# Mamba-plus-MoE layer: the state loop's exponential and pad copy are issued one step ahead

## The chip, the cores and the metric

The kernel runs as one program on all 8 cores of a Trainium2 chip. The cores exchange nothing; each works on half of one sequence. The metric is the time of the slowest core, in microseconds (us) on the device.

Names of the engines in the rows: PE is TensorE (PEld its weight loads), DVE is VectorE, ACT is ScalarE, POOL is GpSimd, SP is SyncE. Here SP only issues DMAs, and POOL only issues DMAs.

## The reference

```python
# per sequence, d_inner = 2048, 16 states, 4096 positions
xi, res = split(x @ W_in)
xi = silu(causal_conv4(xi) + conv_b)
Bm, Cm = split(xi @ W_xproj)
delta = softplus(xi @ W_dt + b_dt)
A = -exp(A_log)                                  # 16 values
def step(h, inp):
    dA = exp(d_i[:, None, :] * A[None, :, None])
    h = h * dA + d_i * B_i * u_i                 # for each of 16 states
    y_i = sum(h * C_i, axis=states)
y = (ys + xi * D_param) * silu(res)
x = layernorm(x + y @ W_out)
# then softmax router (top 2 of 16 experts of 1024x1024) + 2 shared experts
x = layernorm(x + x + routed + shared)
```

## The kernel before

**Stages.** Each core computes 4096 positions of one sequence, of which it outputs 2048. The first 2048 only bring the recurrent state to the right value (or are zeros, for the first half of a sequence). Time is cut in 16 chunks of 256 positions (TA). A position's 2048 channels lie as 16 tiles (CT) of 128 partitions, so a chunk of one quantity is a 128x4096 f32 tile. The stages are: projection and convolution (to about 790 us); the state stage, lines 496 to 742, of which this document speaks; the output projection, layernorm and router; and the mixture of experts. Barriers stand between them.

**The state stage.** Its loop is `for ch in range(NCH)` (line 620, chunks 0 to 15) around `for n in range(NST)` (line 644, steps 0 to 15, one for each state). Chunks 8 to 15 are "real" (line 622): they also produce output. A step n does this:

- ACT: `dA[n%2] = exp(A[n] * d)` (line 653), 128x4096 into one of two buffers `dA_b`. It waits until the scan that last read the buffer is done (`dA_used`, line 652).
- ACT: the pad copy (line 658). It puts the 16 state values that the chunk before left for state n (`carry`) into column 0 of every channel tile of `dBu_b`. It waits for the scan before (`prev_scan`), which read the same tile.
- DVE: `dBu = du * B[n]` (line 665), 128x4096, the rest of that tile.
- DVE: the scan (line 679) `h = dA*h + dBu` over 128x4112; it waits for the pad copy (`actn`, line 678), which is later in ACT's program than the exponential.
- ACT: the carry copy (line 685), last column of `h` into `carry`; it waits for this step's scan.
- In real chunks only, DVE: `y_acc = h * C[n]` (line 696), and PE adds it up over the states in PSUM with 8 identity matmuls (line 701).

Every engine executes its own program in order, and the helper class `Chain` (line 110) makes each DVE and ACT operation wait for its predecessor; all of their rows therefore carry line 121, and one tells them apart by tiles.

**The side work in chunks 0 to 6.** While chunk ch runs its 16 steps, PE computes `delta` of the chunks 2ch+2 and 2ch+3, in 16 groups, one issued at each step (`a2_group`, line 541): a slab of `W_dt` (1 MB in SBUF, two slab buffers) comes in by a DMA from POOL, 34 matmuls use it, and ACT evacuates the two PSUM banks (`a2_evac`, line 575) with an Exp into `g_b` and a Ln into `sres_b`. The evacuations are put into ACT's program at the head of a step, by the list `a2_target` (line 627): none at steps 0 to 3, one at each of steps 4 to 11, two at each of steps 12, 13 and 14, one at step 15, and the last one behind step 15 (line 707). The group issued at step n takes the pair of banks that evacuation n-4 frees. Evacuation 7 (at step 11) and the last one are followed by the store `d_sp<-sres_b` from POOL, ahead of the next slab loads in POOL's program. Chunk 7 has steps without side work.

**Between chunks.** SP's program has, at step 1 of a chunk that isn't real, the load of the next `u_b`, and at step 15 (lines 672 to 677): wait for the last exponential (`dfree_A`, it read `d_b`), load the next `d_b` (2 MB); wait for the last `dBu` product (`dufree_V`), load the next `Bb_b` (2 MB, 16 rows broadcast to all partitions). A next real chunk also loads `Cb_b` behind the last product (lines 713 to 717), and, after the product with `sres_b` (line 731), `u_b` and `sres_b`. The next chunk begins with `du = d * u` on DVE (line 637), which waits for all of these loads at once (`ev_cur`).

Of the kernel before, what the change touches and what calls it, by code (L numbers as in the profile page):

```python
# [12 lines left out]
AF = mybir.ActivationFunctionType  # L13
# [4 lines left out]
NST = 16  # L18
# [7 lines left out]
CT = C2 // 128  # L26
# [102 lines left out]
def build_nc(debug=False, phases=5):  # L129
# [39 lines left out]
    A_bc = sb("A_bc", [128, NST], F32)  # L169
# [14 lines left out]
    carry = sb("carry", [128, NST * CT], F32)  # L184
# [12 lines left out]
    cA = Ctr(es, nc, "cA")  # L197
    cV = Ctr(es, nc, "cV")
# [8 lines left out]
    def emit(_):  # L207
        te = nc.tensor
        ve = Chain(nc.vector, cV)
        se = Chain(nc.scalar, cA)  # L210
# [57 lines left out]
        def emit_ln(in_b, out_b, W, sq_b, stat, mu_bc, rs_bc):  # L268
# [14 lines left out]
            for dt_i in range(DT):  # L283
# [47 lines left out]
                            in_=W_in.rearrange("(k p) c -> p k c", p=128)[:, :, 0:C2]), 16)  # L331
        cL.inc(ge.dma_start(out=wres[:].rearrange("p (k c) -> p k c", c=C2),
                            in_=W_in.rearrange("(k p) c -> p k c", p=128)[:, :, C2:2 * C2]), 16)
        cL.inc(ge.dma_start(out=cvd[:].rearrange("p (i n) -> p i n", n=128),
                            in_=convd.rearrange("i p n -> p i n")), 16)
        cL.inc(ge.dma_start(out=wxp[:].rearrange("p (k c) -> p k c", c=32),
                            in_=W_xproj.rearrange("(k p) c -> p k c", p=128)), 16)
# [4 lines left out]
                            in_=b_dt.rearrange("(c p) -> p c", p=128),  # L342
                            allow_slow_non_contiguous=True), 16)
        cS.inc(sy.dma_start(out=cvb_c[:],
                            in_=conv_b.rearrange("(c p) -> p c", p=128),
                            allow_slow_non_contiguous=True), 16)
        cS.inc(sy.dma_start(out=Dp_c[:],
                            in_=D_param.rearrange("(c p) -> p c", p=128),
                            allow_slow_non_contiguous=True), 16)
        cS.inc(sy.dma_start(out=bsum_c[:],  # L350
                            in_=bs[0].rearrange("(c p) -> p c", p=128),
                            allow_slow_non_contiguous=True), 16)
        cS.inc(sy.dma_start(out=bs_t[:],
                            in_=bs[1].rearrange("(c p) -> p c", p=128),
# [5 lines left out]
                            in_=centT.rearrange("(k p) c -> p k c", p=128)), 16)  # L360
# [33 lines left out]
        for ch in range(NCH):  # L394
            bi = ch % 2
            if xcons[bi]:
                ge.wait_ge(cT.sem, xcons[bi])
            cL.inc(ge.dma_start(
                out=xcb[bi][:].rearrange("p (k t) -> p k t", t=TA),
                in_=xT.rearrange("(k p) t -> p k t", p=128)[:, :, ch * TA:(ch + 1) * TA]), 16)  # L400
# [21 lines left out]
            for cp in range(CT // 2):  # L422
                b = acquire2()
                for ct in (2 * cp, 2 * cp + 1):
# [13 lines left out]
                    in_=pairview(b, TA), func=AF.Silu))  # L438
# [59 lines left out]
        TAp = TA + 1  # L498
# [121 lines left out]
        for ch in range(NCH):  # L620
            a2_done = 0
            real = ch >= NRE
            ev_cur = ev_next
            if ch <= NRE - 2:
                a2_sched = [(2 * ch + 2, mp) for mp in range(CT // 2)] + \
                           [(2 * ch + 3, mp) for mp in range(CT // 2)]
                a2_target = [0, 0, 0, 0, 1, 2, 3, 4, 5, 6, 7, 8, 10, 12, 14, 15]
            else:
                a2_sched = None
            if ch == NRE:  # L630
                zmm_T = a2st['mmend']
                ve.wait_ge(cS.sem, consts_S)
                ve.wait_ge(cA.sem, cA.n)
                cV.inc(ve.tensor_scalar_mul(carry[:], carry[:], flag_col[:]))
                prev_scan = cV.n
            ve.wait_ge(*ev_cur)
            cV.inc(ve.tensor_mul(du_b[:], d_b[:], u_b[:]))
            dumult_V = cV.n
            se.wait_ge(*ev_cur)
            se.wait_ge(cV.sem, pad_V)  # L640
            if ch + 1 < NCH:
                rB.begin()
            dA_used = [0, 0]
            for n in range(NST):
                if a2_sched is not None:
                    while a2_done < a2_target[n]:
                        a2_evac(*a2evacs.pop(0))
                        a2_done += 1
                    a2_group(*a2_sched[n])
                pi = n % 2  # L650
                if dA_used[pi]:
                    se.wait_ge(cV.sem, dA_used[pi])
                cA.inc(se.activation(out=dA3[pi][:, :, 1:TAp], in_=d3,
                                     func=AF.Exp, scale=A_bc[:, n:n + 1]))
                if n == NST - 1:
                    dfree_A = cA.n
                se.wait_ge(cV.sem, prev_scan)
                cA.inc(se.activation(
                    out=dBu3[:, :, 0:1],
                    in_=carry[:, n * CT:(n + 1) * CT].rearrange("p (c o) -> p c o", o=1),  # L660
                    func=AF.Copy))
                actn = cA.n
                bview = Bbc[:, n * TA:(n + 1) * TA].rearrange(
                    "p (o t) -> p o t", o=1).broadcast_to([128, CT, TA])
                cV.inc(ve.tensor_tensor(dBu3[:, :, 1:TAp], du3, bview, ALU.mult))
                if n == 1 and ch + 1 < NCH and not real:
                    syE.wait_ge(cV.sem, dumult_V)
                    rB.dma(syE, out=u_b[:], in_=u_sp[ch + 1])
                if n == NST - 1:
                    dufree_V = cV.n  # L670
                    if ch + 1 < NCH:
                        syE.wait_ge(cL.sem, a2_spill[ch + 1])
                        syE.wait_ge(cA.sem, dfree_A)
                        syE.wait_ge(cV.sem, dumult_V)
                        rB.dma(syE, out=d_b[:], in_=d_sp[ch + 1])
                        syE.wait_ge(cV.sem, dufree_V)
                        bchain(syE, Bb_b, 0, ch + 1)
                ve.wait_ge(cA.sem, actn)
                cV.inc(ve.tensor_tensor_scan(out=h_b[:], data0=dA_b[pi][:],
                                             data1=dBu_b[:], initial=0.0,  # L680
                                             op0=ALU.mult, op1=ALU.add))
                scan_V = cV.n
                prev_scan = scan_V
                se.wait_ge(cV.sem, scan_V)
                cA.inc(se.activation(
                    out=carry[:, n * CT:(n + 1) * CT].rearrange("p (c o) -> p c o", o=1),
                    in_=h3[:, :, TA:TAp], func=AF.Copy))
                dA_used[pi] = cV.n
                if real:
                    cview = Cbc[:, n * TA:(n + 1) * TA].rearrange(  # L690
                        "p (o t) -> p o t", o=1).broadcast_to([128, CT, TA])
                    if zmm_T:
                        ve.wait_ge(cT.sem, zmm_T)
                    if n == 0:
                        ve.wait_ge(*ev_cur)
                    cV.inc(ve.tensor_tensor(y3, h3[:, :, 1:TAp], cview, ALU.mult))
                    if ch == NRE and n == 0:
                        te.wait_ge(cA.sem, a2st['lastA'])
                    te.wait_ge(cV.sem, cV.n)
                    for zb in range(8):  # L700
                        cT.inc(te.matmul(  # L701
                            PP[:, zb * 512:(zb + 1) * 512],
                            sid128[:], y_acc[:, zb * 512:(zb + 1) * 512],
                            start=(n == 0), stop=(n == NST - 1)),
                               1 if zb == 7 else 0)
                    zmm_T = cT.n
            while a2evacs:
                a2_evac(*a2evacs.pop(0))
            if ch + 1 < NCH:
                if ch + 1 == NRE:  # L710
                    syE.wait_ge(cL.sem, a2st['spill'])
                    rB.dma(syE, out=sres_b[:], in_=sres_sp[NRE])
                if ch + 1 >= NRE:
                    if ch + 1 == NRE:
                        syE.wait_ge(cT.sem, a2st['mmend'])
                    syE.wait_ge(cV.sem, cV.n if real else dufree_V)
                    bchain(syE, Cb_b, NST, ch + 1)
            if real:
                ve.wait_ge(cT.sem, zmm_T)
                ve.wait_ge(*ev_cur)  # L720
                for ct in range(CT):
                    cV.inc(ve.scalar_tensor_tensor(
                        out=y_acc[:, ct * TA:(ct + 1) * TA],
                        in0=u_b[:, ct * TA:(ct + 1) * TA],
                        scalar=Dp_c[:, ct:ct + 1],
                        in1=PP[:, ct * TA:(ct + 1) * TA],
                        op0=ALU.mult, op1=ALU.add))
                if ch == NRE:
                    ve.wait_ge(cA.sem, a2st['lastA'])
                ve.wait_ge(cL.sem, gspill_L)  # L730
                cV.inc(ve.tensor_mul(g_b[:], y_acc[:], sres_b[:]))
                ge.wait_ge(cV.sem, cV.n)
                cL.inc(ge.dma_start(out=g_sp[ch], in_=g_b[:]), 16)
                gspill_L = cL.n
                if ch + 1 < NCH:
                    syE.wait_ge(cV.sem, cV.n)
                    rB.dma(syE, out=u_b[:], in_=u_sp[ch + 1])
                    rB.dma(syE, out=sres_b[:], in_=sres_sp[ch + 1])
            if ch + 1 < NCH:
                ev_next = rB.tok()  # L740
# [336 lines left out]
```

## Time and profile before

| | us |
|---|---|
| time, median of 2 runs | 8084.86 (8078.89 to 8090.82) |
| the profiled execution, slowest core | 8089.99 |
| its span in the trace (core 6) | 8088.4 |
| spans of the 8 cores | 8016.9 to 8088.4 |
| busy: DVE / PE / ACT / POOL | 4786.4 / 3794.7 / 1400.7 / 247.2 |

The profile is one execution, seen on the slowest core. "Busy" counts the time in which an engine executes; a row's "idle before" is the time in which the engine stood still ahead of the instruction, with the instruction or transfer that ended the wait behind the arrow. A DMA's time "to landing" runs from its issue to its last byte. The span holds all but 1.6 us of the profiled execution's time.

### The profile page before, as it was taken

To read this page: it belongs to the slowest core of one execution; us is meant where nothing else is said; L and a number is where in the kernel's file an instruction comes from. 1 tells how busy PE (TensorE), PEld (TensorE's weight loads), DVE (VectorE), ACT (ScalarE), POOL (GpSimd) and SP (SyncE) were. 2 spreads that over 40 slices of the span, in tenths; PEclk is the share of its full clock that TensorE was granted. 3 is DMA by queue.
4 is the path that set the end of the run, shared out by engine and by line. 5 is a ranking of instruction groups with operands and counts; after the bars stand their busy time and mean duration, and the time that the engine had idled before them with its cause. 6 is when DMAs were issued, how large, how long until landed. Compare 5 with 4: busy or idle time off the path is not lost.

```text
span 8088.4 us, 43746 instructions; the slowest of 8 cores (8016.9 to 8088.4 us)
## 1 busy us (share of the span) xinstructions
PE 3794.7 (47%) x16512; PEld 2020.6 (25%) x16512; DVE 4786.4 (59%) x1408; ACT 1400.7 (17%) x1270; POOL 247.2 (3%) x252
## 2 busy tenths in 40 slices
PE   3887332232232230344353433535345567676767
PEld 2776221122222220111121211212111123232332
DVE  0211086686687679779797987979773322322222
ACT  0111032232232232112121121212110000000000
POOL 0000000000000000000000000000000000000000
PEclk9998676666666665667676766767667779888888
DMA  6433877576656760130202112020212067676665
GB/s 100 110 115 124 117 119 103 89 107 101 116 82 109 114 99 10 42 57 0 57 0 57 21 36 57 0 57 12 45 48 67 36 122 129 113 127 123 117 128 101
DMA packets 468236, 640.80 MB, mean 79 GB/s; under 512 B 33886, under 2 KB 361950, under 8 KB 448046
## 3 DMA queue, kind: packets, MB, share of 16 engines
q0 software_dynamic: 380816, 352.01, 28.6%
q1 hardware_dynamic: 87214, 285.99, 14.7%
q8 instruction: 135, 2.21, 0.1%
q14 instruction: 71, 0.58, 0.0%
HBM read 796.49 MB, written 134.87 MB: 115 GB/s over the span
## 4 chain that ended last, share of the span: by engine, by line
DVE 50%; DMA 20%; PE 15%; ACT 7%; another core or an unknown queue 5%; issue 3%; SPq 1%; DVEq 0%; ACTq 0%; POOLq 0%; POOL 0%
DVE h_b L121 27%; DVE dBu L121 9%; DMA wr<-WrT 9%; DVE y_acc L121 8%; ACT dAb L121 4%; PE PP L981 3%; DMA sres_b<-sres_sp 2%; PE PP L412 2%; DMA wr<-WsT 1%; PE PP L467 1%; PE PP L802 1%; PE PP L427 1%; DMA Cb_b<-W_dt 1%; DMA gbc_b<-gbc_b 1%
## 5 line engine op out<-in xcount | busy, mean ns | idle before, releaser
L121 DVE TENSOR_TENSOR_SCAN h_b<-dAb,dBu 128x4112 f32<-128x4112 f32 x256 | 2233.6, 8725 | 246.1 <-ACT dBu L121 226.1
L701 PE MATMUL PP<-y_acc,sid 128*128 128x512 f32 x2048 | 1192.5, 748 | 1831.9 <-DVE y_acc L121 1831.9
L563 PE MATMUL PP<-y_acc,Cb_b 128*128 128x256 bf16 x4096 | 681.4, 339 | 1512.6 <-DMA Cb_b<-W_dt 862.6
L121 DVE TENSOR_TENSOR dBu<-du_b,Bb_b 128x4096 f32<-128x4096 f32 x256 | 1132.8, 4425 | 26.7
L701 PEld LDWEIGHTS PP<-y_acc,sid 128*128 128x128 f32 x2048 | 488.4, 246 | 2535.5 <-issue 2535.5
L121 ACT ACTIVATE dAb<-d_b,A_bc 128x4096 f32<-128x4096 f32 x256 | 950.5, 3713 | 792.9 <-DMA sres_b<-sres_sp 414.4
L981 PE MATMUL PP<-ue,wr 128*128 128x512 bf16 x4096 | 923.4, 388 | 211.5 <-DVE ue L121 112.5
L563 PEld LDWEIGHTS PP<-y_acc,Cb_b 128*128 128x128 bf16 x4096 | 486.3, 121 | 1683.9 <-issue 1541.1
L981 PEld LDWEIGHTS PP<-ue,wr 128*128 128x128 bf16 x4096 | 404.4, 100 | 732.1 <-issue 279.3
L121 DVE TENSOR_TENSOR y_acc<-h_b,Cb_b 128x4096 f32<-128x4096 f32 x128 | 566.5, 4426 | 13.7 <-DVE h_b L121 0.5
L121 ACT ACTIVATE carry<-h_b 128x16 f32<-128x16 f32 x256 | 58.7, 229 | 2927.7 <-DVE h_b L121 2927.7
L121 DVE TENSOR_TENSOR du_b<-d_b,u_b 128x4096 f32<-128x4096 f32 x16 | 70.8, 4425 | 754.2 <-DMA Bb_b<-bc_hbm 489.9
L121 DVE SCALAR_TENSOR_TENSOR ue<-u_b,ones,gbc_b 128x4096 bf16<-128x4096 f32 x32 | 143.5, 4484 | 380.8 <-PE PP L981 260.2
L121 DVE SCALAR_TENSOR_TENSOR ue<-u_b,ones,u2b_b 128x4096 bf16<-128x4096 f32 x32 | 143.5, 4484 | 369.1 <-PE PP L981 355.5
L412 PE MATMUL PP<-xcb,wi 128*128 128x256 bf16 x2048 | 249.6, 288 | 150.5 <-DMA xcb<-xT 116.3
L121 DVE CAST xiraw<-PP 128x512 bf16<-128x512 f32 x128 | 88.5, 692 | 371.8 <-DMA sres_sp<-sres_b 189.1
L121 ACT ACTIVATE sres_b<-u_b 128x4096 f32<-128x4096 f32 x4 | 14.5, 3616 | 1463.2 <-DMA ffnin_sp<-u_b 1463.2
L412 PEld LDWEIGHTS PP<-xcb,wi 128*128 128x128 bf16 x2048 | 209.9, 103 | 189.4 <-issue 155.9
L97 POOL DMA_DIRECT2D Cb_b<-W_dt x128 | 146.4, 1145 | 1501.0 <-PE PP L567 1500.1
L121 DVE SCALAR_TENSOR_TENSOR u_b<-PP,bsum_c,u_b 128x512 f32<-128x512 f32 x32 | 24.0, 750 | 236.6 <-PE PP L981 233.3
L427 PE MATMUL PP<-xiraw,cvd 128*128 128x256 bf16 x1024 | 141.0, 272 | 20.0 <-DVE xiraw L121 20.0
L121 ACT ACTIVATE u_b<-PP 128x512 f32<-128x512 f32 x128 | 76.4, 597 | 337.5 <-PE PP L431 337.2
(104 smaller groups left out, 1963.9 us busy)
## 6 DMA issues: line engine op xcount, KB each, us to landing
Cb_b<-W_dt POOLq DMA_DIRECT2D x128, 1024.0 KB, 12.1
wr<-WrT POOLq DMA_DIRECT2D x64, 2048.0 KB, 14.8
u_sp<-u_b SPq DMA_DIRECT2D x20, 2048.0 KB, 7.4
u_b<-u_sp SPq DMA_DIRECT2D x20, 2048.0 KB, 18.5
d_sp<-sres_b POOLq DMA_DIRECT2D x16, 2048.0 KB, 11.9
d_b<-d_sp SPq DMA_DIRECT2D x16, 2048.0 KB, 9.5
Bb_b<-bc_hbm SPq DMA_DIRECT2D x16, 2048.0 KB, 41.6
xib_sp<-xib_b SPq DMA_DIRECT2D x16, 1024.0 KB, 8.7
```

Of the source, the lines that this page charges most:

```text
L97: eng.dma_start(**k).then_inc(self.sems[self.i], 16)
L121: inst = fn(*a, **k)
L412: cT.inc(te.matmul(pb[bb][:, 0:TA], wi[:, kt * C2 + mt * 128: kt * C2 + (mt + 1) * 128], xcb[bi][:, kt * TA:(kt + 1) * TA], start=(kt == 0 ...
L427: cT.inc(te.matmul(pb[bb][:, 0:TA], cvd[:, (tap * 16 + ct) * 128:(tap * 16 + ct + 1) * 128], xr3[:, ct, tap:tap + TA], start=(tap == 0), s ...
L467: cT.inc(te.matmul(pb[bb][:, 0:TA], wres[:, kt * C2 + mt * 128: kt * C2 + (mt + 1) * 128], xcb[bi][:, kt * TA:(kt + 1) * TA], start=(kt == ...
L563: cT.inc(te.matmul(pb[bb][:, 0:TA], slab[:, kt * 256 + i * 128: kt * 256 + (i + 1) * 128], xib2[:, kt * TA:(kt + 1) * TA], start=(kt == 0) ...
L701: cT.inc(te.matmul(PP[:, zb * 512:(zb + 1) * 512], sid128[:], y_acc[:, zb * 512:(zb + 1) * 512], start=(n == 0), stop=(n == NST - 1)), 1 i ...
L802: cT.inc(te.matmul(pb[b][:, 0:TC], wout[:, kt * D + mt * 128: kt * D + (mt + 1) * 128], gb_par[par][:, kt * TC:(kt + 1) * TC], start=(kt = ...
L981: cT.inc(te.matmul(pb[banks_d[dt_i]][:, 0:TC], wr_b[wi_][:, kt * D + dt_i * 128: kt * D + (dt_i + 1) * 128], mov[:, kt * TC:(kt + 1) * TC] ...
```

## The change

The exponential and the pad copy of step n+1 are issued within step n. For ACT the order within a step was: evacuations, exponential n, pad n, (wait for scan n) carry n. It becomes: evacuations, exponential n+1, (wait for scan n) carry n, pad n+1. Exponential 0 and pad 0 of a chunk are issued ahead of the step loop. The waits of each of them stay as they were: an exponential waits for the scan that last read its buffer, which for n+1 is scan n-1; a pad copy waits for the scan before. `dfree_A`, on which SP's load of `d_b` waits, is now the count of an exponential issued in step 14. Nothing is computed otherwise than before, and no tile is added.

```diff
@@ -641,6 +641,25 @@
             dA_used = [0, 0]
+
+            def emit_dA(n):
+                pi = n % 2
+                if dA_used[pi]:
+                    se.wait_ge(cV.sem, dA_used[pi])
+                cA.inc(se.activation(out=dA3[pi][:, :, 1:TAp], in_=d3,
+                                     func=AF.Exp, scale=A_bc[:, n:n + 1]))
+                return cA.n
+
+            def emit_pad(n):
+                se.wait_ge(cV.sem, prev_scan)
+                cA.inc(se.activation(
+                    out=dBu3[:, :, 0:1],
+                    in_=carry[:, n * CT:(n + 1) * CT].rearrange("p (c o) -> p c o", o=1),
+                    func=AF.Copy))
+                return cA.n
+
+            emit_dA(0)
+            actn = emit_pad(0)
             for n in range(NST):
@@ -648,18 +667,6 @@
                 pi = n % 2
-                if dA_used[pi]:
-                    se.wait_ge(cV.sem, dA_used[pi])
-                cA.inc(se.activation(out=dA3[pi][:, :, 1:TAp], in_=d3,
-                                     func=AF.Exp, scale=A_bc[:, n:n + 1]))
-                if n == NST - 1:
-                    dfree_A = cA.n
-                se.wait_ge(cV.sem, prev_scan)
-                cA.inc(se.activation(
-                    out=dBu3[:, :, 0:1],
-                    in_=carry[:, n * CT:(n + 1) * CT].rearrange("p (c o) -> p c o", o=1),
-                    func=AF.Copy))
-                actn = cA.n
@@ -681,11 +688,17 @@
                 scan_V = cV.n
                 prev_scan = scan_V
+                dA_used[pi] = cV.n
+                if n + 1 < NST:
+                    dn = emit_dA(n + 1)
+                    if n + 1 == NST - 1:
+                        dfree_A = dn
                 se.wait_ge(cV.sem, scan_V)
                 cA.inc(se.activation(
                     out=carry[:, n * CT:(n + 1) * CT].rearrange("p (c o) -> p c o", o=1),
                     in_=h3[:, :, TA:TAp], func=AF.Copy))
-                dA_used[pi] = cV.n
+                if n + 1 < NST:
+                    actn = emit_pad(n + 1)
```

## Rows read from the trace of the kernel before

**Rows 1.** Page, part 1: busy us, share of the span and instructions of each engine.
```profile
PE 3794.7 (47%) x16512; PEld 2020.6 (25%) x16512; DVE 4786.4 (59%) x1408; ACT 1400.7 (17%) x1270; POOL 247.2 (3%) x252
```

**Rows 2.** Page, part 4: the chain that ended last, by engine.
```profile
DVE 50%; DMA 20%; PE 15%; ACT 7%; another core or an unknown queue 5%; issue 3%; SPq 1%; DVEq 0%; ACTq 0%; POOLq 0%; POOL 0%
```

**Rows 3.** Waits of DVE in the state stage (1032 to 6030 us): total, times, longest.
```profile
DVE du_b L121 <- DMA Bb_b<-bc_hbm: 322.6, 7, 59.1
DVE h_b L121 <- ACT dBu L121: 226.1, 87, 63.5
DVE du_b L121 <- DMA sres_b<-sres_sp: 219.1, 7, 35.1
...
DVE du_b L121 <- DMA Cb_b<-bc_hbm: 45.2, 1, 45.2
```

**Rows 4.** Line 121's instructions: count, ns min/median/max, first and last start.
```profile
L121 DVE TENSOR_TENSOR dBu<-du_b,Bb_b x256: 4424/4425/4427, 965.4 to 5987.0; 128x4096 f32<-128x4096 f32 x128
L121 ACT ACTIVATE dAb<-d_b,A_bc x256: 3708/3712/3722, 1029.1 to 5982.9; 128x4096 f32<-128x4096 f32 x128
L121 ACT ACTIVATE dBu<-carry x256: 229/230/233, 1032.9 to 5986.7; 128x16 f32<-128x16 f32 x128
L121 DVE TENSOR_TENSOR_SCAN h_b<-dAb,dBu x256: 8723/8725/8726, 1033.3 to 5991.6; 128x4112 f32<-128x4112 f32 x128
L121 ACT ACTIVATE carry<-h_b x256: 228/229/234, 1042.2 to 6000.4; 128x16 f32<-128x16 f32 x128
...
L121 ACT ACTIVATE g_b<-PP x128: 597/597/599, 820.6 to 3004.3; 128x512 f32<-128x512 f32 x128
L121 ACT ACTIVATE sres_b<-g_b x128: 629/630/632, 821.3 to 3005.0; 128x512 f32<-128x512 f32 x128
L121 DVE TENSOR_TENSOR y_acc<-h_b,Cb_b x128: 4425/4426/4426, 3311.6 to 6000.4; 128x4096 f32<-128x4096 f32 x128
```

**Rows 5.** Windows, du to last scan, of chunks 1 and 7: us, busy, clock, DMA.
```profile
1323.30:1563.50 240.20, 214.82 (x33) 0.68 0.64 101
...
3028.10:3247.80 219.70, 214.82 (x33) 0.50 0.06 19
```

**Rows 6.** Timeline of DVE in chunk 1: scans 2, 3 and 4 (start us, us).
```profile
1359.24 8.73 DVE L121 TENSOR_TENSOR_SCAN h_b<-dAb,dBu 128x4112 f32<-128x4112 f32 x1
...
1372.63 8.72 DVE L121 TENSOR_TENSOR_SCAN h_b<-dAb,dBu 128x4112 f32<-128x4112 f32 x1
...
1387.45 8.72 DVE L121 TENSOR_TENSOR_SCAN h_b<-dAb,dBu 128x4112 f32<-128x4112 f32 x1 [1.56 <-ACT dBu L121]
```

**Rows 7.** Timeline of ACT, chunk 1, step 12: the pad behind two evacuations.
```profile
1506.95 0.23 ACT L121 ACTIVATE dBu<-carry 128x16 f32<-128x16 f32 x1
```

**Rows 8.** Timeline of PE, chunk 1: the two halves of group 13.
```profile
1520.33 3.57 PE L563 MATMUL PP<-y_acc,Cb_b 128*128 128x256 bf16 x16 [7.16 <-DMA Cb_b<-W_dt]
...
1523.91 2.12 PE L563 MATMUL PP<-y_acc,Cb_b 128*128 128x256 bf16 x16
```

**Rows 9.** Timeline of SP's DMA issues at the end of chunk 1.
```profile
1554.23 0.32 SPq L97 DMA_DIRECT2D d_b<-d_sp  x1
1554.67 0.37 SPq L97 DMA_DIRECT2D Bb_b<-bc_hbm  x1
```

**Rows 10.** DMA issues, 1554 to 1622 us (chunk 1 to 2): KB, us to landing.
```profile
d_b<-d_sp SPq DMA_DIRECT2D x1, 2048.0 KB, 9.8
Bb_b<-bc_hbm SPq DMA_DIRECT2D x1, 2048.0 KB, 66.6
```

**Rows 11.** DMA issues, 3238 to 3294 us (chunk 7 to 8): KB, us to landing.
```profile
d_b<-d_sp SPq DMA_DIRECT2D x1, 2048.0 KB, 10.4
Bb_b<-bc_hbm SPq DMA_DIRECT2D x1, 2048.0 KB, 34.2
...
Cb_b<-bc_hbm SPq DMA_DIRECT2D x1, 2048.0 KB, 42.5
```

**Rows 12.** DMA issues, 3910 to 3985 us (chunk 9 to 10): KB, us to landing.
```profile
Cb_b<-bc_hbm SPq DMA_DIRECT2D x1, 2048.0 KB, 45.7
```

## The prediction, made before the changed kernel was run

> **What bounds the kernel now.** I read the busy shares first. No engine is full over the whole span: DVE has 59% [rows 1]. The chain that ended last goes half through DVE [rows 2], and DVE's work is in the state stage, so I read that stage. Its waits on DVE [rows 3] are the whole case: 226.1 us ahead of the scan, released by ACT's pad copy, and 322.6 + 219.1 + 45.2 = 586.9 us ahead of `du`, released by loads between the chunks. Then the windows of two chunks that run the same 33 DVE instructions [rows 5]: both are busy for 214.82 us, but chunk 1, with side work, takes 240.2 us and chunk 7, without it, 219.7 us. So within a chunk DVE sets the pace, and what is above 219.7 is ACT being late.
>
> Why it is late can be seen step by step. The reader should set three scans beside one another [rows 6]. Scan 3 starts 13.39 us behind scan 2; scan 4, the first with an evacuation at its step's head, starts 14.82 us behind scan 3 and has waited 1.56 us for the pad. Between two scans ACT runs, all behind the scan that has just ended: carry 0.23, evacuation 0.60 + 0.63, exponential 3.71, pad 0.23 [rows 4], with about 0.09 us between each two: 5.4 + 0.4 = 5.8 us. DVE covers only one `dBu` product of 4.43 us [rows 4]. The difference is the wait. With two evacuations it is one more pair, 1.23 + 0.18 = 1.4 us: the pad of step 12 begins at 1506.95 and ends at 1507.18 [rows 7], 2.97 us behind the product. Without an evacuation ACT needs 4.6 us counted from the scan, and the step is 13.39 instead of the 8.73 + 4.43 + two gaps of 0.1 = 13.35 that DVE alone would take. In real chunks the y product lies there too, 4.43 + 4.43 = 8.9 us of cover, so nothing waits.
>
> **The change, part by part.**
>
> *Exponential ahead of the carry wait.* Exponential n+1 needs only scan n-1 and its buffer's turn; it will run beside scan n. What is left behind scan n is carry 0.23 and pad 0.23 with their gaps, 0.7 us, under a product of 4.43 us. So the wait for the pad goes. Per chunk with side work there are 9 steps with one evacuation and 3 with two: 9 x 1.41 + 3 x 2.8 = 21.1 us of step time; by the windows it is 240.2 - 219.7 = 20.5. I take the windows: 7 chunks (0 to 6) x 20.5 = 144 us. The step floor, 13.39 to 13.35, gives 15 x 8 x 0.05 = 6 us more, in the 8 chunks that aren't real. Of the 226.1 us, the one wait of 63.5 [rows 3] is ACT working off the evacuations ahead of chunk 0; nothing of it is touched. **Term 1: -150 us.** Bounds: 144 and 156.
>
> *What ACT's new order queues.* The evacuations of step n now come ahead of exponential n+1, carry n and pad n+1. An evacuation that waits for PE would hold these. ACT's budget: pad n is done 0.7 us behind scan n-1; DVE wants exponential n+1 only when product n, scan n and product n+1 are through, 17.8 us behind that scan. Two evacuations and the exponential need 2.8 + 3.8 + 0.7 = 7.3 us. So an evacuation may wait 10 us for PE before DVE feels it. The tightest group is 13: its slab comes late, since store and slabs are queued behind evacuation 7, and its matmuls end at 1523.91 + 2.12 = 1526.0 [rows 8], and evacuation 13 is second at step 14. The pad of step 12 begins at 1506.95 [rows 7], so that step's first evacuation began 3.8 + 2.8 = 6.6 us before it, at 1500.3, and that of step 11 a step of 14.8 us earlier, at 1485.5: group 13 is done 40.5 us behind it. Three new steps and a first evacuation are 3 x 13.35 + 1.4 = 41.5 us. So PE is just in time, and 10 us are in hand. Cost: 0; if groups 11 to 14 came over 10 us later than now, each further us would cost one.
>
> *Exponential beside the scan.* No row shows ACT at work during a scan. The nearest: the `dBu` product has the exponential beside it at every step but step 0 of a chunk, and its 256 durations are 4.424 to 4.427 us; the y product likewise [rows 4]. So I take 0. The far bound is that the two exclude each other: 256 x 3.71 = 950 us. The Trainium skill (SBUF — State Buffer, "Who interferes with whom") gives ScalarE a read and a write port of its own and only lets VectorE and GpSimd block each other; by it this cost is 0 as well, and the sum stays.
>
> *Loads between the chunks.* SP's issue of the `d_b` load waits for exponential 15. Now it is issued at 1554.23, and `Bb_b` 0.44 us behind it [rows 9], though product 15 was done by then: the scan behind it waits 1.56 us for the pad here too, as in [rows 6]. `d_b` lands in 9.8 us and `Bb_b` in 66.6 us [rows 10], both on SP's queue, so that `Bb_b` stands behind `d_b`; `du` begins right when `Bb_b` has landed. With the change exponential 15 ends about 13 us earlier, before product 15 starts; `d_b` is then nearly or wholly landed when `Bb_b` is issued, and `Bb_b` is issued some 1.5 us earlier against the product. If `d_b` held `Bb_b` up for its full 9.8 us, a boundary gains up to 11 us; if `Bb_b` is slow for other reasons (34.2 us to landing at the boundary from 7 to 8 [rows 11], 66.6 here), part of it comes back as contention. I take 8.5 for each of the 7 boundaries into chunks 1 to 7: **Term 2: -60 us**, bounds 0 and -77. Into chunk 8 the same queue holds `d_b`, `Bb_b`, `sres_b` and `Cb_b`, and `Cb_b` lands last, 42.5 us after its issue [rows 11]; without the 10.4 us of `d_b` in front I take **Term 3: -8 us**, bounds 0 and -10. Into chunks 9 to 15 (7 boundaries) `d_b` is also early, by a whole real step, but `Bb_b` follows it by 4.8 us already, and what ends the wait is `sres_b`, issued behind the last product, itself behind `Cb_b` (45.7 us [rows 12]). At most 5 us of `d_b` stand in front of `Bb_b`; I take 2 each: **Term 4: -14 us**, bounds 0 and -35.
>
> *The earlier `d_b` load against side work.* It now runs while group 15's slab comes in. That slab may come up to 9.8 us later; evacuation 15 stands behind the last scan, 13 us further on, so this is covered.
>
> **Sum.** 8090 - 150 - 60 - 8 - 14 = 7858 us against the profiled execution, which is 5 us above the median of the runs shown; I predict 7855.
>
> **The rivals.**
>
> *The boundaries give nothing back.* `Bb_b` takes 66.6 us at one boundary and 34.2 at another for the same bytes, so its pace is set by something other than `d_b`, maybe the other cores' loads. Then only term 1 stays: 8085 - 150 = 7935. For it: the spread of landing times. Against it: the same queue, and the 10.4 us of `d_b` in front of the fast one too.
>
> *The boundaries give more.* Landing of `Bb_b` gets 11 us earlier each time and the real chunks gain their 5: 8085 - 156 - 77 - 10 - 35 = 7807.
>
> *Side work becomes the bound.* The 14.8-us step gave PE and the slabs 11% more time than the 13.35-us step will. The Trainium skill (DMA: Bandwidth & Descriptors, "Issuing engines are not separate DMA queues") says that DMAs of all issuing engines run on the same 16 DMA engines and interleave; by it the earlier `d_b` load of 2 MB slows the slab under way. As a mechanism of this kernel: groups 11 to 15 slip until an evacuation waits beyond its 10 us and takes back, say, the three double steps, 3 x 2.8 x 7 = 59 us: 7914. For it: group 13 is within 1 us of its evacuation. Against it: 10 us in hand, and the DMA share of chunk 1 is 0.64 [rows 5], not full.
>
> *Slower: scan and exponential hinder each other.* All 256 scans now have 3.71 us of exponential beside them. From 235 / 256 = 0.9 us per scan the change loses; full exclusion gives 7855 + 950 = 8805. For it: no row shows the pair. Against it: the products, which read two tiles as the scan does, did not move by 3 ns.
>
> **Chances and range.** Forecast 0.65 (7820 to 7895); boundaries give nothing or little 0.13 (7895 to 7945); more 0.10 (7795 to 7820); side work 0.07 (7880 to 7960); scans slowed 0.05, of which 0.03 slower. To hold 8 in 10 I take 7810 to 7930. About 2% (162 us, that is 7923) is what a measurement here can tell: faster by more 0.85, within 0.12, slower 0.03.
>
> **What would show it.** In the profile after: scan-to-scan 13.35 us at all steps of chunks 0 to 7; the wait "scan for the pad copy" down from 226 to about 64 us; chunks with side work 218 to 219 us from `du` to the last scan; scans still 8.725 us; `d_b` issued within step 14 and `du`'s waits on `Bb_b` down from 322.6 by about 60. I am wrong in the mechanism if the scans get longer, if ACT is seen waiting for PE ahead of an exponential and DVE for that one, and in the sizes if the waits between chunks stay at 587 us.

## The result, and the profile after

| | before | after |
|---|---|---|
| time, median of the runs | 8098.78 us (8078.89 to 8115.21, 8 runs) | 7999.40 us (7983.02 to 8021.19, 9 runs) |
| ratio | | 0.988 (95%: 0.9863 to 0.9897) |
| profiled execution | 8089.99 us, core 6 slowest | 8008.96 us, core 0 slowest |

The change makes the kernel 1.2% faster, about 99 us. I had forecast 230 us, and a range that ended at 7930. In some executions the cores of one die have a lower granted clock and take over 1% longer than the others; no ratio in this document counts them.

Where the time went can be told in one table. Each core's span is cut at the first `du` of the state stage, at the last scan of each chunk, and at the `du` behind it; a "pause" is the time from the end of a chunk's last scan to the next chunk's `du`. The figures are means over the 8 cores, in us.

| part | before | after | difference | forecast |
|---|---|---|---|---|
| ahead of the first `du` | 957 | 959 | +2 | 0 |
| inside the 16 chunks, `du` to the end of the last scan | 4253 | 4097 | -156 | -150 |
| pauses into chunks 1 to 7 | 308 | 306 | -2 | -60 |
| pause into chunk 8 | 46 | 55 | +9 | -8 |
| pauses into chunks 9 to 15 | 396 | 452 | +56 | -14 |
| behind the last scan | 2092 | 2100 | +8 | 0 |
| mean span of the cores | 8052 | 7969 | -83 | -232 |

The steps did what they were to do. The waits of DVE in the state stage of the changed kernel (core 0; total us, times, longest):

```profile
DVE du_b L121 <- DMA Bb_b<-bc_hbm: 318.9, 7, 56.5
DVE du_b L121 <- DMA sres_b<-sres_sp: 276.2, 7, 44.3
...
DVE h_b L121 <- ACT dBu L121: 62.9, 1, 62.9
DVE du_b L121 <- DMA Cb_b<-bc_hbm: 54.5, 1, 54.5
```

Beside [rows 3]: 86 of the 87 waits of the scan for the pad copy are gone, and the one left is the one of chunk 0 that the change doesn't touch. But the waits of `du` for the loads are 649.6 us together, where they were 586.9. Windows of chunks 1 and 7 of the changed kernel, `du` to the end of the last scan (us, DVE busy, clock, DMA share, GB/s), to be set beside [rows 5]:

```profile
1316.20:1534.50 218.30, 214.84 (x33) 0.69 0.75 115
2892.10:3110.60 218.50, 214.76 (x33) 0.50 0.10 26
```

A chunk with side work now takes as long as one without. Timelines of ACT and DVE around step 13 of chunk 1 show the new order:

```profile
1494.53 0.23 ACT L121 ACTIVATE carry<-h_b 128x16 f32<-128x16 f32 x1 [6.18 <-DVE h_b L121]
1494.85 0.23 ACT L121 ACTIVATE dBu<-carry 128x16 f32<-128x16 f32 x1
1495.18 0.60 ACT L121 ACTIVATE g_b<-PP 128x512 f32<-128x512 f32 x1
...
1498.00 3.71 ACT L121 ACTIVATE dAb<-d_b,A_bc 128x4096 f32<-128x4096 f32 x1
```
```profile
1485.66 8.73 DVE L121 TENSOR_TENSOR_SCAN h_b<-dAb,dBu 128x4112 f32<-128x4112 f32 x1
1494.49 4.42 DVE L121 TENSOR_TENSOR dBu<-du_b,Bb_b 128x4096 f32<-128x4096 f32 x1
1499.02 8.72 DVE L121 TENSOR_TENSOR_SCAN h_b<-dAb,dBu 128x4112 f32<-128x4112 f32 x1
```

Pad 13 is done at 1495.08, four microseconds before the product that the scan needs as well, and scan to scan is 13.36 us. The exponential (1498.00 to 1501.71) lies 2.7 us deep in the scan that starts at 1499.02, and the scan is as long as ever. That is not so at every step: on core 0 an exponential runs beside 80 of the 256 scans, 139 us in all, nearly all of them in steps with evacuations; at the other steps it begins some 0.7 us behind the scan before and is done within the product, as it was before the change. All scans of the kernel (count, then ns min/median/max):

```profile
L121 DVE TENSOR_TENSOR_SCAN h_b<-dAb,dBu x256: 8724/8725/8726, 1055.2 to 5918.5; 128x4112 f32<-128x4112 f32 x128
```

What is left is the pauses. Into chunk 10 (issues between 3785 and 3881 us of core 0, with KB and us to landing), where [rows 12] had 45.7 us for `Cb_b`:

```profile
Bb_b<-bc_hbm SPq DMA_DIRECT2D x1, 2048.0 KB, 48.2
Cb_b<-bc_hbm SPq DMA_DIRECT2D x1, 2048.0 KB, 55.9
```

The same 2 MB of the same tensor, in a stretch where ACT's order changes nothing on DVE, take 10 us more. In real chunks the steps are 17.89 us in both kernels. So a change that was only to let ACT run ahead made transfers slower.

### The profile page after: what moved, and what is told of

The parts are those of the page before. It is cut to its first block, busy times and chain, and to the rows that moved or that the text cites. A ratio compares the mean times of both kernels' runs of the same rounds, so it can differ in the third digit from the quotient of the medians.

```text
span 8007.4 us, 43746 instructions; the slowest of 8 cores (7935.2 to 8007.4 us)
## 1 busy us (share of the span) xinstructions
PE 3817.7 (48%) x16512; PEld 2036.2 (25%) x16512; DVE 4786.7 (60%) x1408; ACT 1401.1 (17%) x1270; POOL 247.3 (3%) x252
## 4 chain that ended last, share of the span: by engine, by line
DVE 55%; DMA 19%; PE 16%; another core or an unknown queue 5%; issue 2%; SPq 1%; ACT 1%; DVEq 0%; ACTq 0%; POOLq 0%; POOL 0%
DVE h_b L121 28%; DVE dBu L121 14%; DMA wr<-WrT 9%; DVE y_acc L121 8%; PE PP L994 4%; PE PP L412 2%; DMA sres_b<-sres_sp 2%; PE PP L467 2%; PE PP L427 2%; DMA wr<-WsT 1%; PE PP L815 1%; SPq L97 1%; DMA gbc_b<-gbc_b 1%; DMA Cb_b<-W_dt 1%
## 5 line engine op out<-in xcount | busy, mean ns | idle before, releaser
L121 ACT ACTIVATE carry<-h_b 128x16 f32<-128x16 f32 x256 | 58.7, 229 | 2754.8 <-DVE h_b L121 2754.8
L121 ACT ACTIVATE sres_b<-u_b 128x4096 f32<-128x4096 f32 x4 | 14.5, 3616 | 1454.9 <-DMA ffnin_sp<-u_b 1454.9
```

What stands on the lines that cost most here:

```text
L121: inst = fn(*a, **k)
```

## The experiments

**What could do that.** Theory P: `Bb_b` and `Cb_b` are broadcasts (each partition reads the same 16 rows of 1 KB), they are slow, and the two cores of a pair (0 and 1, 2 and 3, and so on) slow each other's when theirs overlap; the change lets the cores of a pair come closer in time. The Trainium skill (HBM Reference, opening line and "Specifications") says that the memory is shared by pairs of NeuronCores. The traces agree: a broadcast of the partner lowers a core's rate and one of another pair's core does not (79 packets in a us to 47, and 79 against 80, counted below). Theory Q: the `d_b` load, now issued earlier in every chunk (by 17 us in real ones), is itself what disturbs the broadcasts.

To begin with the traces at hand: in real chunks of the kernel before, the cores of a pair start chunk 8 between 43 and 44 us apart; in the changed kernel 29 to 32 us. As its real chunks go on the distance grows to between 40 and 44 us, and the pause falls from about 70 us to between 57 and 62.

### The new order in one half of the chunks

`ahead_0to7` and `ahead_8to15` issue ahead in chunks 0 to 7 or 8 to 15 only:

```diff
-            emit_dA(0)
-            actn = emit_pad(0)
+            ahead = AHEAD(ch)          # ch < NRE, or ch >= NRE
+            if ahead:
+                emit_dA(0)
+                actn = emit_pad(0)
...
                 pi = n % 2
+                if not ahead:
+                    dn = emit_dA(n)
+                    if n == NST - 1:
+                        dfree_A = dn
+                    actn = emit_pad(n)
```

> The new order of ACT in chunks 0 to 7 only; chunks 8 to 15 as before the change. What is to be told apart is why the pauses between the real chunks (into chunks 9 to 15) went from 390 to 450 us in sum. Theory P (the two cores of a pair slow each other's B and C broadcasts, and the change brings them closer in time, about 31 us apart at chunk 9 instead of 44): the pauses into 9 to 15 stay near those of the changed kernel, 440 to 470 us in sum, and the ratio to before is 0.986 to 0.990. Theory Q (the d_b load that the new order issues earlier in real chunks is itself what slows the broadcasts): the sum is back at 385 to 415, and the ratio is about 0.980.

> The new order of ACT in chunks 8 to 15 only; chunks 0 to 7 as before the change. Theory P: the pair comes into chunk 9 about 44 us apart as before, so the pauses into 9 to 15 sum to 385 to 415 us and the ratio is 1.000 within 0.003. Theory Q: the pauses sum to 440 to 470 us and the ratio is 1.007.

Measured: 0.9889 (0.9871 to 0.9906) with the new order in chunks 0 to 7, and 1.0001 (0.9982 to 1.002) with it in chunks 8 to 15. The pauses into chunks 9 to 15, means of the cores: 445 us where the real chunks are untouched, 401 us where only they are changed. The waits of `du` in the state stage, first of `ahead_0to7` (core 6), then of `ahead_8to15` (core 0):

```profile
DVE du_b L125 <- DMA Bb_b<-bc_hbm: 315.5, 7, 56.5
DVE du_b L125 <- DMA sres_b<-sres_sp: 268.0, 7, 43.0
```
```profile
DVE du_b L125 <- DMA Bb_b<-bc_hbm: 327.3, 7, 59.8
...
DVE du_b L125 <- DMA sres_b<-sres_sp: 201.1, 7, 31.7
```

Both came out as P has it. The gain and nearly all of the loss come from chunks 0 to 7: the pauses into chunks 9 to 15 grow by what happened before them. The early `d_b` load in real chunks is worth at most some 8 us in seven pauses (401 against 396 with nothing else changed, 452 against 445 in the changed kernel), and so Q has fallen for them as the main cause.

### The `d_b` load held back

`late_db`: SP waits for product 15 in chunks 0 to 7, and for the y product of step 14 in real chunks.

```diff
                         syE.wait_ge(cA.sem, dfree_A)
-                        syE.wait_ge(cV.sem, dumult_V)
+                        syE.wait_ge(cV.sem, dufree_V - 1 if real else dufree_V)
```

> The changed kernel with the d_b load held back to about its old place: SP waits for product 15 in chunks 0 to 7, and for the y product of step 14 in real chunks. Theory P: the pauses are those of the changed kernel within 5 us each, ratio 0.986 to 0.993. Theory Q: the pauses into 9 to 15 are back at 385 to 415 us in sum, ratio 0.980 to 0.983.

Measured: 0.987 (0.9831 to 0.9908), the changed kernel's ratio. But the pauses are not the changed kernel's, as P's expectation had them: they are 336 us into chunks 1 to 7 (306), and 405 into 9 to 15 (452). Taken alone the second number speaks for Q. It doesn't decide, for a reason that I had not foreseen in writing P's expectation: the pairs of this kernel start chunk 8 between 36 and 40 us apart and chunk 12 between 41 and 49, further than the changed kernel's. What it does show is that the early load is worth 30 us in the pauses 1 to 7.

With these five kernels there are 140 cases (7 pauses of 4 pairs each) of a distance (between the `du` of a pair's two cores, each counted from its own span's start, at the chunk ahead of the pause) and a pause (mean of the two cores):

| us apart | 25-30 | 30-35 | 35-40 | 40-45 | 45-50 |
|---|---|---|---|---|---|
| cases | 3 | 20 | 29 | 44 | 43 |
| mean pause, us | 71.0 | 68.1 | 63.1 | 58.5 | 55.0 |
| least and most | 70.6, 71.4 | 65.2, 70.7 | 60.3, 65.5 | 55.6, 62.2 | 52.3, 58.7 |

(One case at 50 us had 53.4.) The correlation is -0.98, and the line has 0.89 us more pause for each us that the pair is closer. It is one line for all five kernels, whatever their order and whenever `d_b` is loaded: the pauses of `late_db` lie on it to 0.1 us in the mean, those of each other kernel to 0.6. The distance was never set on purpose, it only came out differently. Why the change brings the pairs closer no run shows.

The packets show the slowing itself. Into chunk 10 of the changed kernel core 1's `Cb_b` lands at 3833.6 us, and core 0's `Bb_b` is issued at 3801.7. The queue of these loads on core 1 (packets, MB, busy share), from 3780 to 3800 us, with no broadcast of core 0 under way, and from 3806 to 3826, beside core 0's:

```profile
q1 hardware_dynamic: 1412, 1.43, 56.1%
```
```profile
q1 hardware_dynamic: 1243, 1.27, 101.8%
```

And on core 0, from 3806 to 3826 us, beside core 1's, and from 3845 to 3865, with none of core 1 under way:

```profile
q1 hardware_dynamic: 834, 0.85, 66.1%
```
```profile
q1 hardware_dynamic: 1927, 1.96, 78.2%
```

Counted over all pauses into chunks 9 to 15 (1 KB packets that a core completes in a us while a broadcast of its own is under way, from 2 us behind its issue to its landing; from the packets' times in the traces of all cores):

| kernel | partner's broadcast under way | not under way | overlap per core, us |
|---|---|---|---|
| before | 35 | 84 | 19 |
| after | 47 | 79 | 139 |
| `ahead_0to7` | 44 | 82 | 122 |
| `ahead_8to15` | 45 | 81 | 23 |
| `late_db` | 42 | 83 | 42 |

A core of another pair has no such hold: in the changed kernel, while the partner's is not under way, the rate is 79 with a broadcast of the core two numbers further under way and 80 without. As an estimate from these rows, the overlap costs a core 139 x (1 - 47/79) = 56 us in the changed kernel and 19 x (1 - 35/84) = 11 in the kernel before; the difference of 45 us is most of the 56 that these pauses grew by. Each core's times are counted from its own first instruction, and no trace shows that the two cores of a pair start together; but core 0 goes from 157 packets in 5 us (3835 to 3840) to 266, 387 and 538 in the next three such stretches, right behind the landing on core 1.

### Another place in memory for B and C

`bc_hbm` has 32 rows (B and C of 16 states), 16 KB apart, one row for all 4096 positions. A broadcast takes 1 KB of each of 16 rows, 128 times. `after_bc` is the changed kernel with the same numbers stored chunk by chunk, so that a partition's piece is one of 16 KB:

```diff
-    bc_hbm = dm("bc_hbm", [32, TV], F32, spk)
+    bc_hbm = dm("bc_hbm", [NCH, 32, TA], F32, spk)
...
-        cS.inc(sy.dma_start(out=bc_hbm, in_=BC_buf[:]), 16)
+        cS.inc(sy.dma_start(out=bc_hbm.rearrange("c n t -> n c t"),
+                            in_=BC_buf[:].rearrange("n (c t) -> n c t", t=TA)), 16)
...
-                   out=buf[:].rearrange("p (n t) -> p n t", n=NST),
-                   in_=bc_hbm[r0:r0 + NST, win * TA:(win + 1) * TA][None]
-                   .broadcast_to([128, NST, TA]))
+                   out=buf[:],
+                   in_=bc_hbm[win, r0:r0 + NST, :].rearrange(
+                       "n t -> (n t)")[None].broadcast_to([128, NST * TA]))
```

> The changed kernel with B and C stored chunk by chunk, so that each partition's 16 rows of a chunk are one contiguous piece of 16 KB and the broadcast loads go in large packets instead of 2048 of 1 KB. If the number of packets sets the pace: Bb_b lands some 10 to 15 us after its issue instead of 49, pauses into chunks 1 to 7 fall from 45 to about 20 us, those into 9 to 15 from 65 to about 43 us, where the u and sres loads behind the last product bound them; ratio to before about 0.94. If instead all partitions reading the same place in memory sets it: landing times as in the changed kernel, ratio 0.988.

Measured: 7470.89 us, 0.9223 (0.9189 to 0.9256). DMA issues of this kernel, medians to landing:

```profile
Bb_b<-bc_hbm SPq DMA_DIRECT2D x16, 2048.0 KB, 8.8
...
Cb_b<-bc_hbm SPq DMA_DIRECT2D x8, 2048.0 KB, 7.2
```

and its waits of DVE in the state stage:

```profile
DVE du_b L121 <- DMA sres_b<-sres_sp: 112.3, 7, 16.2
...
DVE du_b L121 <- DMA Cb_b<-bc_hbm: 11.4, 1, 11.4
DVE du_b L121 <- DMA Bb_b<-bc_hbm: 6.1, 6, 1.7
```

The pauses into chunks 1 to 7 are gone (4.6 us in all seven together, as the mean of the cores, where 306 were), better than my 20 us each. Those into 9 to 15 are 43 to 47 us on every core, though the pairs are here only 7 to 14 us apart. In `before_bc` below they are 43 to 46 us at 20 to 28 us apart, where the line above, drawn out to there, would have over 70: with short broadcasts the distance has no hold.

Two kernels tell the size of the packets from the distance of the rows. `after_pitch` moves the rows 17 KB apart and changes nothing else; `after_row1k` stores chunk by chunk, with rows 1088 bytes apart, so that packets stay at 1 KB:

```diff
# after_pitch
-    bc_hbm = dm("bc_hbm", [32, TV], F32, spk)
+    bc_hbm = dm("bc_hbm", [32, TV + 256], F32, spk)[:, 0:TV]
# after_row1k
+    bc_hbm = dm("bc_hbm", [NCH, 32, TA + 16], F32, spk)[:, :, 0:TA]
```

> The changed kernel with the B and C rows 17 KB apart in memory instead of 16 KB; the broadcasts still go in 1 KB packets. If the power-of-two distance of the rows makes the broadcasts slow: Bb_b lands in well under 49 us (15 to 30), pauses into 9 to 15 near 45 us. If the 1 KB packets do: nothing changes, Bb_b 49 us, time within 30 us of the changed kernel's 8000.

> The changed kernel with B and C stored chunk by chunk as in the fast layout, but each row padded by 64 bytes, so that the 16 rows of a load lie in 17 KB of memory and still go as 1 KB packets. If the spread of the rows over memory is what counts: as fast as the chunk-wise layout, about 7470 us, Bb_b landing in about 9 us. If the packets of 1 KB are what counts: as the changed kernel, Bb_b 49 us, about 8000 us.

Measured, one execution each: 7498.66 and 7501.59 us, so the pitch alone does it, and more fully than the 15 to 30 us that I expected for `Bb_b`. DMA queue and issues of `after_pitch`:

```profile
q1 hardware_dynamic: 87214, 285.99, 11.6%
...
Bb_b<-bc_hbm SPq DMA_DIRECT2D x16, 2048.0 KB, 8.2
...
Cb_b<-bc_hbm SPq DMA_DIRECT2D x8, 2048.0 KB, 8.8
```

The queue of the changed kernel, on its page:

```profile
q1 hardware_dynamic: 87214, 285.99, 15.9%
```

Packets and bytes are equal to the last one; their time is less, and `Bb_b` lands in 8.2 us (11.2 in `after_row1k`), where the changed kernel's median is 49.0. So the 1 KB packets cost next to nothing, and 16 KB from row to row cost everything. The Trainium skill (DMA: Bandwidth & Descriptors, "Latency and other measured facts") lists copies that halve their rate at row distances of 4 MiB and more and recover with 4 KiB of padding, and calls the cause an inference. These runs show the same cure at 16 KB, for reads of the same rows by all partitions (49.0 to 8.2 us). Which part of the memory is hit no run here shows.

### The change where the broadcasts are short

`before_bc` is the kernel before the change with the layout of `after_bc`; `late_db_bc` is `after_bc` with `d_b` held back as above.

> The kernel before the change with B and C stored chunk by chunk (one 16 KB piece per partition and load). With short broadcasts nothing between the chunks should depend on how far the two cores of a pair are apart. Theory P: the change is then worth what it takes out of the steps, 156 us (7 chunks of 22 us and chunk 7's 1 us), so this kernel should take about 7471 + 156 = 7627 us, ratio to before 0.942. If the gain of the change is lost for another reason than the pair: only some 97 us slower than the changed kernel in this layout, 7568 us, ratio 0.935.

> The changed kernel in the chunk-wise layout, with the d_b load held back to its old place. It prices the earlier d_b load without the slow broadcasts. If that load is all that the change does between the chunks: pauses into chunks 1 to 7 as in the kernel before in this layout, 33 and 51 us in sum on the two cores of a pair, against 3 to 6 us with the early load; those into 9 to 15 stay at 312; time about 7471 + 42 = 7513 us, ratio to before 0.928. If the denser side work also costs between the chunks, as the pauses of the held-back kernel in the old layout suggest (322 and 351 us against 290 and 326), the sums are over 60 us, and the ratio is 0.930 or more.

Measured: `before_bc` 7672.21 us, 0.9481 (0.9449 to 0.9513); so here the change is worth 7672 - 7471 = 201 us, 2.6% (209 us by the two ratios). That is more than either expectation had, since the one that took P left out the early load, which the traces show beside the steps. In the traces some 15 us of it lie ahead of the first `du` (925 against 910), where the change does nothing. Of `late_db_bc` the table has cores 4 to 7 alone, whose granted clock, 0.752 to 0.757, is near that of `after_bc` (0.753 to 0.759); cores 0 to 3 had 0.732 to 0.737:

| means of the cores, us | before_bc | late_db_bc | after_bc |
|---|---|---|---|
| inside the chunks | 4252 | 4098 | 4097 |
| pauses into 1 to 7 | 42 | 47 | 4.6 |
| pause into 8 | 14 | 14 | 11 |
| pauses into 9 to 15 | 313 | 311 | 312 |

The early load is worth 43 us in the pauses 1 to 7, 3 into chunk 8, and nothing between real chunks. The sums into 1 to 7 are 39 to 54 us on these cores, which is the first expectation (33 and 51) and not the second (over 60). `late_db_bc` took 7556.51 us, 0.9318 (0.9259 to 0.9376), 77 to 86 us above `after_bc`, as the second expectation had it; but its pauses explain only 46 of these, and the rest goes with the clock: its one execution with 0.751 or more on every core took 7521.58 us, 51 above `after_bc`, and in the other four the slowest core had 0.732 to 0.738.

### A version that beats both

`after_bc` is 7.8% faster than the kernel before. One more kernel, `after_bc_quarters`, does the output sum, the product with `sres_b` and the loads of the next `u_b` and `sres_b` in four quarters:

```diff
+                for q in range(4):
+                    for ct in range(4 * q, 4 * q + 4):   # scaled add, as before
...
+                    cV.inc(ve.tensor_mul(g_b[:, qs], y_acc[:, qs], sres_b[:, qs]))
+                    syE.wait_ge(cV.sem, cV.n)
+                    rB.dma(syE, out=u_b[:, qs], in_=u_sp[ch + 1][:, qs])
+                    rB.dma(syE, out=sres_b[:, qs], in_=sres_sp[ch + 1][:, qs])
```

> The changed kernel in the chunk-wise layout; in addition the output product of a real chunk and the loads of the next u_b and sres_b go in four quarters, so that three quarters of these loads run under the product. The pause into chunks 9 to 15, 45 us in the chunk-wise layout, consists of y product 4.4, PE's tail 9.4, scaled adds 9.2, product 4.4 and about 16 us of loads; with quarters about 4 us of loads are left: 33 us. Seven times 12 = 84 us: about 7390 us, ratio to before 0.912. If the loads are bound by something else than their place: 0.922 as the chunk-wise layout alone.

Measured: 7421.21 us, 0.9177 (0.9163 to 0.9191). I had expected 7390 and 0.912. The pause into a real chunk is 37.7 us and not 33; the wait of `du` for the loads is 55.5 us in seven (core 3), 8 each, where I had reckoned with 4.

## Why the prediction was wrong

**Term 1, the steps: right.** -156 us inside the chunks against -150, at the edge of its bounds (144 and 156), and 13.36 us from scan to scan against 13.35. One reading in it was wrong without harm to the sum: "All 256 scans now have 3.71 us of exponential beside them". Only 80 do (core 0), 22 of them for more than 2 us, and the other exponentials run beside the product as before. Those 80 scans are 8.724 to 8.726 us long like all others, so the 0 held, as far as 139 us of company can tell, and that rival fell. The trace agrees with the rule that the prediction cites from the Trainium skill (SBUF — State Buffer, "Who interferes with whom").

**ACT's queue: right inside the chunks, not at their end.** Before the change ACT never waited for PE once the chunks ran; on core 0 of the changed kernel it does, 13 times, 74.1 us in sum. Within the chunks these waits are at most 4.8 us, so group 13 and its neighbours were at the edge, DVE felt none of it, and the cover of 10 us was there. But the last evacuation, which I had called covered, came late: it stands behind the last scan, and in four of the seven chunks it waited 8.5 to 16.1 us for group 15 (ACT's timeline, core 0, the longest two):

```profile
2360.53 0.60 ACT L121 ACTIVATE g_b<-PP 128x512 f32<-128x512 f32 x1 [16.07 <-PE PP L567]
...
2622.58 0.60 ACT L121 ACTIVATE g_b<-PP 128x512 f32<-128x512 f32 x1 [15.44 <-PE PP L567]
```

It is seen on cores 0, 3, 5 and 7, in each pair the one that runs behind; on the others the longest such wait is 7.4 us. So the store and the next slabs, which go out behind it, moved deeper into the pause there (the store, on core 0, up to 18.7 us behind the last scan, 2.7 before the change). The `d_b` load too went out later than I had reckoned: 14.5 to 19.3 us ahead of the end of the last scan on core 0, not the 22.1 us that chunk 7, without evacuations, shows.

**Term 2, pauses into chunks 1 to 7: the step that failed first.** I took 8.5 us for each, "bounds 0 and -77". Two things happened where I saw one. The early load did its part: 30 us against the held-back load in the old layout, 43 in the new one. But with the load held back, these pauses are 336 us in the changed kernel and 308 in the kernel before; the new order of ACT, with the steps closer together, made them 28 us longer, and that took the gain back. With short broadcasts this loss is 5 us (47 against 42), so it too is a loss in the slow broadcasts. (Some 3 us of it, in either layout, are that the held-back kernels issue the loads 0.4 us later against the last scan than the kernel before.) A part is the pair again: by the count above, the overlap in these pauses is 68 us per core in the kernel before, at 31 packets in a us against 43, and 106 in `late_db`, at 30 against 41, which as an estimate costs 18 and 28 us, 10 of the 28. Whether the rest comes from the late group 15 or from the partner's side work stays open.

**Terms 3 and 4: wrong in sign.** I bounded both at 0, since nothing is added to these pauses. Into chunk 8 the pause grew by 9 us, into chunks 9 to 15 by 56. The step that failed is the assumption that a load takes what it took before unless its own issue or its own queue changes. The pace of these loads was low by the rows' distance of 16 KB, and it fell further, from 79 packets in a us to 47, whenever the other core of the pair had its own broadcast under way; and in the changed kernel the cores were closer: 44 us apart before, 30 after. By the line above, 14 us closer are 12 us more in each pause at first. Terms 2, 3 and 4 missed by 58, 17 and 70 us, 145 of the 149 between forecast and the mean core's -83. Of these, 52 are gains of the early load that did not come (82 forecast in the three terms, 30 measured), and 93 are the slowing that I had put at nothing (28, 9 and 56).

**The rivals.** "The boundaries give nothing back" named "maybe the other cores' loads" and was nearest to the mechanism, but I priced it as a gain withheld (7935) and not as a loss (7999 measured). The evidence for it was in view: 66.6 us at one boundary and 34.2 at another, for the same 2 MB [rows 10, 11]. A transfer whose time varies by two at the same work should have been asked what it depends on before anything was built on its length; and its 60 GB/s and less, beside the 200 of the `d_b` load in the same queue (2 MB in 9.8 us), should have been asked about in any case. "Side work becomes the bound" was not what happened inside the chunks, where DVE never waited for it.

Worked out anew with what the runs show: -156 in the steps, -2 (30 gained, 28 lost) into chunks 1 to 7, +9 into 8, +56 into 9 to 15, +10 elsewhere, -83 for the mean core. In the layout without slow broadcasts my sum of -232 would have come near the -201, but in part by luck: the terms are there -154, -38, -3 and 0, and 15 of the rest lie ahead of the state loop.

## What to carry to other kernels

When a transfer in the profile takes very different times for the same bytes, find out what it depends on before you price a change by it: here it was the distance of the rows in memory, and with it the distance in time to the other core of the pair, which moved with the change. A shorter step frees only what the next wait leaves: of 156 us, 63 went back into pauses that this change doesn't touch. And a broadcast or strided read of a few rows that lie a large power of two apart (16 KB here; no run tried another) is worth one run with padded rows: here one changed line gave five times what the change under study did.

## What the hardware showed that I had not expected

- Broadcasts of 16 rows of 1 KB to 128 partitions (2 MB): median 49.0 us to landing with rows 16 KB apart, 8.2 us with rows 17 KB apart, 11.2 us with rows 1088 bytes apart, and 8.8 us as one contiguous piece of 16 KB; packets and bytes of the first two were the same.
- With the slow broadcasts, each us that the two cores of a pair are closer in time goes with 0.89 us more in the pause between real chunks (140 cases, 29 to 50 us apart, pauses of 52 to 71 us). In the changed kernel a core completes 47 of the 1 KB packets in a us while its partner's broadcast is under way and 79 while it is not; the broadcast of a core of another pair makes no difference (79 and 80). With the fast layouts the pause is 43 to 47 us at 7 to 28 us apart.
- ACT's exponential on 128x4096 did not slow DVE's scan of 128x4112, which reads two SBUF tiles: the 80 scans with an exponential beside them (139 us together, core 0) are 8.724 to 8.726 us long, as are the 176 without.
